# Feed-forward gate and up products: seven block products in place of eight

## The reference

```python
Wg = dequant_nvfp4(gate_W_packed, gate_scales)   # 4096 x 512
Wu = dequant_nvfp4(up_W_packed, up_scales)       # 4096 x 512
Wd = dequant_nvfp4(down_W_packed, down_scales)   # 512 x 4096
gate = jnp.einsum('th,nh->tn', xt, Wg)
up = jnp.einsum('th,nh->tn', xt, Wu)
gelu = jnp.tanh(0.7978845608028654 * (gate + 0.044715 * gate ** 3)) * gate * 0.5 + gate * 0.5
inter = gelu * up
out = jnp.einsum('tn,hn->th', inter, Wd)
```

## Time and profile before

| what | value |
|---|---|
| median of three runs | 1390.36 us (1389.65 to 1391.3) |
| the profiled execution | 1391.3 us |
| its span in the profile | 1389.3 us |
| TensorE busy | 1361.1 us, 98% |
| VectorE busy | 1053.3 us, 76% |
| ScalarE busy | 417.6 us, 30% |
| GpSimd busy | 244.3 us, 18% |

### The profile page before, as it was taken

The page is one execution under the profiler, slowest core; times in us unless marked ns, Lnnn a source line. Parts: engine busy times, 40 slices in busy tenths (PEclk is TensorE's granted clock), DMA queues, the critical chain, the costliest instruction groups (busy, mean ns, idle before and its releaser), DMA issues.

```text
span 1389.3 us, 18724 instructions
## 1 busy us (share of the span) xinstructions
PE 1361.1 (98%) x7132; PEld 1122.5 (81%) x7132; DVE 1053.3 (76%) x1698; ACT 417.6 (30%) x669; POOL 244.3 (18%) x136
## 2 busy tenths in 40 slices
PE   8899999997999999999999999999999999999999
PEld 5788888886788888888888888888888888888887
DVE  7899998886677676868686867777776868686845
ACT  5333443332232222222232222222222222222221
POOL 1444444451110110101011101010110101010100
PEclk9999999999999999999999999999999999999999
DMA  9000000000000000100000100000000000000002
GB/s 320 22 1 1 17 16 16 1 1 1 16 31 16 31 31 16 31 15 30 15 30 27 34 15 30 15 30 15 30 28 17 30 15 30 15 30 16 1 31 91
DMA packets 21783, 40.29 MB, mean 29 GB/s; under 512 B 2661, under 2 KB 2917, under 8 KB 21605
## 3 DMA queue, kind: packets, MB, share of 16 engines
q1 hardware_dynamic: 21060, 39.47, 8.6%
q10 hardware_dynamic: 672, 0.13, 0.0%
HBM read 35.40 MB, written 4.19 MB: 29 GB/s over the span
## 4 chain that ended last, share of the span: by engine, by line
PE 94%; DVE 3%; issue 1%; ACT 1%; DVEq 0%; ACTq 0%
PE bank L948 29%; PE bank L950 29%; PE bank L949 29%; PE bank L962 2%; PE bank L1038 1%; PE bank L1055 1%; PE bank L1187 1%; PE bank L1045 1%; DVE x1l L709 1%; PE bank L1066 0%; PE bank L1005 0%; PE bank L1004 0%; PE bank L1017 0%; DVE acc L800 0%; DVE hl L834 0%
## 5 line engine op out<-in xcount | busy, mean ns | idle before, releaser
L948 PE MATMUL bank<-x1h,wh 128*128 128x512 f32 x1024 | 398.9, 390 | 1.4 <-DVE x1l L709 1.4
L949 PE MATMUL bank<-x1l,wh 128*128 128x512 f32 x1024 | 398.5, 389 | 0.0
L950 PE MATMUL bank<-x1h,wl 128*128 128x512 f32 x1024 | 398.4, 389 | 0.0
L882 POOL TENSOR_TENSOR wl<-wf,wh 128x1024 fp32r<-128x1024 f32 x48 | 114.9, 2395 | 856.9 <-ACT wh L377 856.9
L948 PEld LDWEIGHTS bank<-x1h,wh 128*128 128x128 f32 x1024 | 192.4, 188 | 41.5 <-issue 1.6
L949 PEld LDWEIGHTS bank<-x1l,wh 128*128 128x128 f32 x1024 | 192.4, 188 | 40.0
L950 PEld LDWEIGHTS bank<-x1h,wl 128*128 128x128 f32 x1024 | 192.3, 188 | 39.9
L809 DVE SCALAR_TENSOR_TENSOR hx<-hx,bank 128x512 f32<-128x512 f32 x128 | 87.9, 687 | 156.6 <-ACT hx L461 156.6
L948 PE MATMUL bank<-wh,hh 128*128 128x512 f32 x512 | 200.6, 392 | 3.2 <-DVE x1l L709 3.2
L949 PE MATMUL bank<-wl,hh 128*128 128x512 f32 x512 | 200.4, 391 | 0.0
L950 PE MATMUL bank<-wh,hl 128*128 128x512 f32 x512 | 200.4, 391 | 0.0
(11 more groups left out here) (117 smaller groups left out, 1476.2 us busy)
## 6 DMA issues: line engine op xcount, KB each, us to landing
pk<-packed_dram SPq DMA_DIRECT2D x48, 256.0 KB
sc<-scales_dram SPq DMA_DIRECT2D x48, 256.0 KB
out_dram<-acc SPq DMA_DIRECT2D x16, 256.0 KB, 2.1
acc<-x_dram SPq DMA_DIRECT2D x3, 1024.0 KB, 13.5
w_in<-wq_dram SPq DMA_DIRECT2D x2, 512.0 KB, 4.8
w_in<-wk_dram SPq DMA_DIRECT2D x2, 512.0 KB, 6.5
...
```

The costliest lines, as they stand in the source:

```text
L882: nc.gpsimd.tensor_tensor(wl[par][:, bass.ds(u, 1), :].rearrange("p a w -> p (a w)"), wf[:].rearrange("p a w -> p (a w)"), wh[par][:, bass ...
L948: pe.matmul(dst, w_h, x_h, start=start, stop=False)
L949: pe.matmul(dst, w_h, x_l, start=False, stop=False)
L950: return pe.matmul(dst, w_l, x_h, start=False, stop=stop)
```

## The change

Gate and up of 256 features and 1024 tokens are now one product of 2 x 2 blocks each: the weights A (features in halves of 128, inputs in halves of 256) and the transposed tokens B (inputs in halves, tokens in halves of 512). Instead of eight block products there are seven, of sums of blocks (Winograd's form of Strassen's scheme): A11 B11, A12 B21, S1 T1, S2 T2, S3 T3, S4 B22 and A22 T4. A block product is six matmuls of 512 columns (`product`). The results C11, C12, C21, C22 are sums of products. Some sums are formed by going on in the same bank (`GA`, `UA`), after ScalarE has copied the bank at three points (`g_copy`, `u_copy`), and some by VectorE (`total`: three for gate, three for up).

The unit of work is now a pair: a block `q` and a half of the tokens `p`, 32 pairs. The down product has eight rows of 128 tokens a pair, each of six matmuls in one of two banks; VectorE adds each row to `acc`. h has four parts with their buffers (`hx`, `hh`, `hl` 0 to 3 are C11, C22, C21, C12).

The seven token operands are formed once: `x1_sums` on GpSimd in eight pieces, 32 groups of up to four transposes, high parts on ScalarE and low parts on VectorE, for all 2048 tokens. The seven weight operands are formed for each unit of gate and up: VectorE scales into four slots of `ws` (output in two contiguous halves now), GpSimd makes the four sums there (`unit_sums`), ScalarE the high parts and GpSimd the low parts of all seven (`wide_hi`, `wide_lo`, two pieces of 896 columns). Down has two pieces of 512. There is one set of weight buffers instead of two: up and down of a block are prepared in the first pair and at the start of the second, gate of the next in the second; `pk`, `sc` and `nib` are single too. At the start, two small loads and the work on them are put in another order.

TensorE's order in a pair, six matmuls each: 1 gate into GA; 2 up of the pair before, into UA; 3 gate into GB; 4 up of the pair before, into UC; 5 gate GA; 6 gate GC; 7 gate GA; 8 down row 0 (of the pair before); 9 gate GA; 10 row 1; 11 gate GC; 12, 13 rows 2, 3; 14 up UA; 15 row 4; 16 up UB; 17 row 5; 18 up UA; 19 row 6; 20 up UC; 21 row 7; 22 up UA.

```diff
+PAIRS = 2 * BLOCKS
+ROWS = TILES // 2
+OPS = 7
+A11, S1, A12, A22, S3, S2, S4 = range(OPS)
+B11, B21, B22, T1, T2, T3, T4 = range(OPS)
+C11, C22, C21, C12 = range(4)
...
+            def unit_sums(k, n):
+
+                pool.wait_ge(dq_f, k + 1)
+                n4 = 4 * n
+                nc.gpsimd.tensor_tensor(part(S3), part(A11), part(S1), ALU.subtract
+                                        ).then_inc(s_sum, 1)
+                nc.gpsimd.tensor_tensor(part(S1), part(S1), part(A22), ALU.add
+                                        ).then_inc(s_sum, 1)
+                pool.wait_ge(s_sum, n4 + 2)
+                nc.gpsimd.tensor_tensor(part(S2), part(S1), part(A11), ALU.subtract
+                                        ).then_inc(s_sum, 1)
+                pool.wait_ge(s_sum, n4 + 3)
+                nc.gpsimd.tensor_tensor(part(S4), part(A12), part(S2), ALU.subtract
+                                        ).then_inc(s_sum, 1)
+
+            def wide_lo(k, hi, lo):
+                for piece in range(2):
+                    pool.wait_ge(dq_hi, 2 * k + piece + 1)
+                    nc.gpsimd.tensor_tensor(lo[:, piece, :, :], ws[:, piece, :, :],
+                                            hi[:, piece, :, :].bitcast(F32), ALU.subtract
+                                            ).then_inc(dq_lo, 1)
+
...
-            def step(q, par_q, tb):
-                if tb >= 1 and not (isinstance(q, int) and q == BLOCKS - 1):
-                    unit_lo(UNITS * (q + 1) + tb - 1, tb - 1, 1 - par_q)
-
-            pairs(pool, step)
+            def pair(q, p):
+                P_ = 2 * q + p
+                first = isinstance(q, int) and P_ == 0
+                ready = isinstance(q, int) and q == 0
+                last = isinstance(q, int) and q == BLOCKS - 1
+                if p == 1 and not ready:
+                    down_lo(3 * q + DOWN)
+                if p == 0 and not ready:
+                    unit_sums(3 * q + UP, 2 * q + UP)
+                    wide_lo(3 * q + UP, wuh, wul)
+                if p == 1 and not last:
+                    unit_sums(3 * q + 3 + GATE, 2 * q + 2 + GATE)
+                if p == 1 and not last:
+                    wide_lo(3 * q + 3 + GATE, wgh, wgl)
+
+            blocks(pool, pair)
...
+            def unit_scale(k):
                 dve.wait_ge(dq_bits, 5 * k + 5)
-                dve.wait_ge(dq_lo, k)
-                s = sc[:, bass.ds(u, 1), :].rearrange("p a w -> p w a")
-                V.scalar_tensor_tensor(out=wf[:].rearrange("p a w -> p w a"),
-                                       in0=nib[:].bitcast(F16).rearrange("p (w a) -> p w a", a=2),
-                                       scalar=16384.0, in1=s.broadcast_to([P, 512, 2]),
+                dve.wait_ge(s_sc, 16 * k + 16)
+                wait(dve, dq_lo, 2 * k)
+                V.scalar_tensor_tensor(out=ws[:, :, 0:4, :].rearrange("p a s m -> p a (s m)"),
+                                       in0=nib.bitcast(F16).rearrange("p (w a) -> p a w", a=2),
+                                       scalar=16384.0,
+                                       in1=sc.unsqueeze(1).broadcast_to([P, 2, 512]),
                                        op0=ALU.mult, op1=ALU.mult).then_inc(dq_f, 1)
...
+                act.wait_ge(g_ps, 7 * P_ + 1)
+                wait(act, h_lo[C11], P_)
+                copy(hx[C11][:], GA, g_copy)
+                if not first:
+                    wait(act, y_ps, 8 * P_ - 8)
+                    high_of(C22, P_ - 1)
+                    if p == 1 and not ready:
+                        act.wait_ge(y_ps, 16 * q)
+                        down_hi(3 * q + DOWN, 0)
+                    high_of(C21, P_ - 1)
+                    if p == 1 and not ready:
+                        down_hi(3 * q + DOWN, 1)
+                act.wait_ge(g_sum, 3 * P_ + 1)
+                square_of(C11, GB, P_)
+                act.wait_ge(g_ps, 7 * P_ + 3)
+                wait(act, u_sum, 3 * P_)
+                copy(cxb[:], GA, g_copy)
+                tanh_of(C11, P_)
+                if first:
+                    ot_hi_(TILES - 1)
+                if not first:
+                    high_of(C12, P_ - 1)
+                act.wait_ge(g_ps, 7 * P_ + 5)
+                wait(act, h_lo[C22], P_)
+                copy(hx[C22][:], GA, g_copy)
+                if p == 0 and not ready:
+                    act.wait_ge(u_ps, 14 * q)
+                    wide_hi(3 * q + UP, 2 * q + UP, wuh, 0)
+                act.wait_ge(g_sum, 3 * P_ + 2)
+                square_of(C22, cxa, P_)
+                act.wait_ge(g_ps, 7 * P_ + 6)
+                wait(act, h_lo[C21], P_)
+                square_of(C21, GA, P_)
+                if p == 0 and not ready:
+                    wide_hi(3 * q + UP, 2 * q + UP, wuh, 1)
+                tanh_of(C22, P_)
...
+            def up_22_21(pair):
+                dve.wait_ge(u_copy, 3 * pair + 3)
+                dve.wait_ge(u_ps, 7 * pair + 5)
+                total(cxa[:], UC, cxa[:], u_sum)
+                dve.wait_ge(u_sum, 3 * pair + 2)
+                prod(C22, cxa, pair)
+                dve.wait_ge(u_ps, 7 * pair + 6)
+                prod(C21, UA, pair)
+
+            def up_12(pair):
+                dve.wait_ge(u_ps, 7 * pair + 7)
+                total(UC[:], UC, cxb[:], u_sum)
+
+                if not (ready and P_ <= 1):
+                    up_22_21(P_ - 1)
+                if p == 0 and not ready:
+                    unit_scale(3 * q + UP)
+                dve.wait_ge(g_ps, 7 * P_ + 2)
+                dve.wait_ge(g_copy, 3 * P_ + 1)
+                total(GB[:], GB, hx[C11][:], g_sum)
+                if not first:
+                    low_of(C22, P_ - 1)
+                    low_of(C21, P_ - 1)
+                    up_12(P_ - 1)
+                arg(C11, GB, P_)
+                if first:
+                    ot_lo_(TILES - 1)
+                if not first:
+                    dve.wait_ge(u_sum, 3 * P_)
+                    prod(C12, UC, P_ - 1)
+                gelu(C11, GB, P_)
+                if not first:
+                    low_of(C12, P_ - 1)
+                if p == 0 and not ready:
+                    unit_bits(3 * q + DOWN)
+                if p == 1 and not last:
+                    unit_bits(3 * q + 3 + GATE)
+                dve.wait_ge(g_copy, 3 * P_ + 3)
+                total(cxa[:], GC, hx[C22][:], g_sum)
+                y(0)
+                arg(C22, cxa, P_)
+                y(1)
+                arg(C21, GA, P_)
+                gelu(C22, cxa, P_)
+                if first:
                     add_x1(TILES - 1)
-                    x1t_lo_(10)
-                    x1t_lo_(11)
                     stats2(2)
-                if at == 1:
-                    for t in range(12, TILES):
-                        x1t_lo_(t)
-                    unit_scale(k, 0)
-
-            pairs(dve, step)
-            add_y(TBS * BLOCKS - 1, TBS - 1, True)
+                x1(16, 17)
+                gelu(C21, GA, P_)
+                dve.wait_ge(g_ps, 7 * P_ + 7)
+                total(GC[:], GC, cxb[:], g_sum)
+                y(2)
+                if p == 1 and not last:
+                    unit_scale(3 * q + 3 + GATE)
+                x1(18, 19)
+                arg(C12, GC, P_)
+                y(3)
+                gelu(C12, GC, P_)
+                y(4)
+                x1(20, 21)
+                dve.wait_ge(u_ps, 7 * P_ + 2)
+                dve.wait_ge(u_copy, 3 * P_ + 1)
+                total(UB[:], UB, cxa[:], u_sum)
+                dve.wait_ge(u_sum, 3 * P_ + 1)
+                prod(C11, UB, P_)
+                y(5)
+                low_of(C11, P_)
+                if p == 1 and not last:
+                    unit_bits(3 * q + 3 + UP)
+                y(6)
+                if p == 0 and not ready:
+                    unit_scale(3 * q + DOWN)
+                y(7)
...
+            def product(dst, w, slot, p, op, start, signal):
+                for a in range(2):
+                    w_h, w_l = w[0][:, a, slot, :], w[1][:, a, slot, :]
+                    x_h, x_l = xoh[p][:, op, a, :], xol[p][:, op, a, :]
+                    pe.matmul(dst[:], w_h, x_h, start=start and a == 0, stop=False,
+                              skip_group_check=True)
+                    pe.matmul(dst[:], w_h, x_l, start=False, stop=False, skip_group_check=True)
+                    ins = pe.matmul(dst[:], w_l, x_h, start=False, stop=a == 1,
+                                    skip_group_check=True)
+                ins.then_inc(signal, 1)
...
+                if p == 0:
+                    pe.wait_ge(dq_lo, 6 * q + 2)
+                if ready:
+                    pe.wait_ge(x1t_lo, 4 * CHUNKS * (p + 1))
+                wait(pe, h_gelu[C21], P_)
+                gate(GA, A11, p, B11, True)
+                if not ready:
+                    up_21(P_ - 1, 1 - p)
+                wait(pe, h_gelu[C11], P_)
+                gate(GB, A12, p, B21, True)
+                if not ready:
```

(48 more changed lines are left out.)

660 lines of the change are left out of this document (380 added, 280 removed).

## The result

The changed kernel took 1395.50 us (median of 6 runs, 1394.34 to 1397.45), the kernel before 1390.62 beside it (6 runs). The ratio is 1.0036, 95% interval [1.0026, 1.0047]: slower by 4.9 us, a third of a per cent, where 6 us faster was forecast.

A forecast was written before the change was run, and what follows sets the result against it. TensorE, 98% busy, was taken as the bound. Block 1 at 393.8, plus 15 x 64.8 = 972, plus 16.7 gave a span of 1382.5 and a time of 1384 us; range 1345 to 1412, likeliest case 1370 to 1400.

The forecast's parts named there:

- The loop: The 15 feed-forward blocks from block 1 on: 64.8 us each against 65.3, halves 34.3 and 30.5.
- slot 7: Seventh place in TensorE's order per half block: waits 1.1 us in first halves, 0.4 in second.
- slot 11: Eleventh place in TensorE's order per half block: in first halves waits 1.85 us for VectorE's sum for C22.
- slot 15: Fifteenth place in TensorE's order: in first halves waits 0.9 us, VectorE adding output row 2 late.
- slot 14: Fourteenth place in TensorE's order: in first halves waits 0.3 us for GpSimd's second up low part.
- Rival A: In the loop most waits don't happen: half the waits gives 1347 us, none 1310; chance 0.18.
- C: Rival: VectorE's scaling stays at 2.05 us, 1408 us; or GpSimd's sums take 1.2, 1402; chance 0.19 together.
- B: Rival: TensorE's clock falls after first-half pauses, 1.6 us lost per block, 1408 us; chance 0.13.
- The lock: VectorE operations without a bank input stand still while GpSimd works, about 15.6 us per block instead of 7.2.
- the Sum: Adding up the whole kernel: block 1 at 393.8, 15 blocks 972, end 16.7, span 1382.5 us.
- waits taken as equal: Before block 1: only counted matmuls and transposes change, -10.1 us, so block 1 starts at 393.8 instead of 403.9.
- tail: After the last pair: two products, eight rows, evacuation, add and store, 16.7 us in all, against 5.8 before.

The follow-up runs named there:

- experiment 7: Changed kernel with GpSimd's weight sums and low parts cut to 4 of 128 columns from block 1 on, all signals kept: 1328.61 us, ratio 0.9550.
- 8: Changed kernel with VectorE's bit operations for the down weights moved late in the first halves of blocks: 1356.02 us, ratio 0.9746.
- 9: Changed kernel, loop reordered so GpSimd's sums and low parts lie over VectorE's bank reads, down's bit operations late too: 1350.64 us, ratio 0.9710.
- 11: Changed kernel with the edits of 9, 1 and Experiment 4, plus up's scaling and copies and GpSimd's sums placed anew: 1327.71 us, again 1327.33.
- 1: Changed kernel with the start-up order of the kernel before: 1391.58 us, ratio 1.0005.
- 2: Kernel before with the changed kernel's start-up order alone: 1395.93 us, ratio 1.0040.
- 3: Changed kernel with only the load order and VectorE's part of the old start-up order, ScalarE's order left as changed: 1393.83 us, ratio 1.0018.
- Experiment 4: Changed kernel with ScalarE's high copies of gate's and up's first weights put earlier in tiles 6 and 8: 1394.46 us, ratio 1.0029.
- 5: Changed kernel with the statistics of tiles 8 to 13 moved from tile 14 into the last tile: 1400.91 us, ratio 1.0074.
- 6: Changed kernel with VectorE's norm of tile 14 ahead of low parts, and TensorE's tile 15 scores ahead of groups 4 to 7: 1399.63 us, ratio 1.0058.
- 12: On top of 11, matmuls whose result nobody reads placed in TensorE's two pauses between tiles 14 and 15: 1325.47 us, ratio 0.9533.
- Experiments 8 to 11: Loop reorderings of the changed kernel: 8, 9, then 9 with the edits of 1 and Experiment 4 (1344.91 us), then 11.

## Why the prediction was wrong

**The loop was right.** Durations: the scaling takes 1.22 us, as I took it. By the rule of the Trainium skill, Vector Engine (DVE) Microarchitecture Reference, "Measured stream behaviour on trn2", my estimate was about 1.1, and the measurement agrees to a tenth. A GpSimd sum takes 0.74 us instead of 0.60, and 1.07 to 1.19 where it meets VectorE's low parts. VectorE's own work per half was forecast at 24.6 of 29.9 us, and in experiment 7, without holds, it is 739 of 900, which is 24.6. Of the pauses, with 0.27 added to each bracket (0.11 of it is the restart, forecast apart as 0.08), slot 7 was forecast 1.1 and 0.4 (1.12 and 0.66 measured), slot 11 1.85 (1.54), slot 15 0.9 (0.96), slot 14 0.3 (0.1). Block 64.39 for 64.8: 15 x 0.41 = 6.2 us better than forecast. Rival A (pauses don't happen) and C (slow scaling or sums) are out. So is B: after these pauses the loop's clock stays at 1.00.

**The lock was right, and makes every pause of the loop.** Experiment 7 takes away GpSimd's columns and every pause goes; 8, 9 and 11 move the meetings and the pauses go with them. The Trainium skill, SBUF — State Buffer, "Who interferes with whom", says that the port pair which VectorE shares with GpSimd is an exclusive lock, and that a VectorE operation with one SBUF input outside the two-port modes does not contend; the trace agrees, down to rows read from a bank (0.68 us beside GpSimd) against low parts (2.18).

**The step that failed is in the Sum: "waits taken as equal".** I took the start-up, the weights' first preparation and the turn from attention to blocks as unchanged but for counted matmuls and transposes, -10.1 us. Measured, block 1 starts 5.8 us later than before, a miss of 15.9:

- start-up order, 5.3 us at tile 1: shown both ways, by 1 (3.9 us less) and 2 (4.9 more). I had seen the reordered start-up in the change and charged nothing for it, although all of GpSimd's first rope would lie over Newton steps: the very lock I priced in the loop. That hold is about half of it; the other half is the place of g2's halves (3).
- tiles 6 to 10, 3.0 us: two low parts of 896 columns, 4.2 us together, hold what VectorE does meanwhile, where one of 1024 took 2.4. Experiment 4 moved it elsewhere and got 1.3 of it back in the trace. Argued from rows, shown only in part. (The tiles around them win 0.3.)
- scores of tile 14 to tile 15, 4.9 us: 12 wide matmuls fewer and 10 transposes more should have made this stretch 1.4 us shorter, and it is 3.5 longer. Its pauses are 2.25, 2.93 and 0.17 us instead of 1.37 and 0.53, and its last transposes run at a granted clock of 0.50. That the missing product is what lays them bare is argued from the rows: two other orders of VectorE's work (5 and 6) only made it worse, and the direct test was not made. A11 B11 needs only B11, 256 inputs of four tiles, but the kernel transposes all seven operands of two tiles at a time and waits for all 16 groups; an order that has B11 ready first could have filled the place again.
- from there to block 1, 3.0 us: by counts (60 wide matmuls fewer, 38 transposes more) it should be 8.7 us shorter and is 5.7. TensorE's idle time is what it was (10.1 us against 9.8), so here waits were equal and the matmuls slower. 12 shows the clock in and behind the turn's pauses to be worth about 1.9 us, most of it here; the rest stays open.

With the 6.2 us won in the loop and a tail of 17.9 us for 16.7 (one more pause of 0.69, in the last pair's up product), the span is 1393.4 for 1382.5. So it is by luck that the time lies between 1370 and 1400: the loop's 6 us hid over a third of the front's 16. The start-up order alone is most of what the kernel lost against before: without it the changed kernel is at 1391.6, level with before; the forecast's 6 us faster needed the other places too.

**What I left out of the rivals** was the best case. I followed the pauses and took the order as given; A's "none: 1310" was priced as luck. Experiments 8 to 11 show it is a choice: the same instructions, set so that GpSimd lies over VectorE's bank reads, are 68 us faster, 5.7 of them from the front.
